# Products nobody reads, behind each group of gathered rows

## The reference

```python
msg = concat([h[src], h[dst]]) @ Mw.T + Mb
s1, s2 = segment_sum(msg, dst), segment_sum(msg * msg, dst)
mx, mn = segment_max(msg, dst), segment_min(msg, dst)
mean = s1 / deg;  var = relu(s2 / deg - mean * mean);  std = sqrt(var + 1e-30)
agg = concat([mx, mn, std, var])
u = concat([h, agg, agg * (logd / 4), agg * (4 / logd)]) @ Uw.T + Ub
u = batch_norm(u * sqrt(1 / N))
h = leaky_relu(u @ mix_w.T + mix_b, 0.01) + h
h = elu(layer_norm(h))
```

## Time and profile before

| | us |
|---|---|
| median of 3 runs | 2159.31 |
| lowest and highest of them | 2149.97, 2159.78 |
| span of the profiled execution | 2141.7 |
| PE busy, share of the span | 682.6, 32% |
| DVE busy | 1096.6, 51% |
| ACT busy | 455.6, 21% |
| POOL busy | 1235.7, 58% |

### The profile page before, as it was taken

How to read it: one execution, slowest core, us unless ns; L and a number is a source line. 1 busy time by engine, 2 the same in 40 slices (tenths; PEclk the granted TensorE clock), 3 DMA queues, 4 the chain that set the end, 5 groups by cost and what they waited for, 6 DMA issues and landing times. The chain is left out here.

```text
span 2141.7 us, 10446 instructions
## 1 busy us (share of the span) xinstructions
PE 682.6 (32%) x2156; PEld 402.8 (19%) x2156; DVE 1096.6 (51%) x2178; ACT 455.6 (21%) x1024; POOL 1235.7 (58%) x1358
## 2 busy tenths in 40 slices
PE   5611233132322470323132232362113322233265
PEld 5311121011111230112111111131101211112122
DVE  8600755464644843445464463572525664466464
ACT  0103321122111154111111111136101221112125
POOL 7673666676666127745675675406756666576504
PEclk9975666565655685566565666686556666656677
DMA  4363333333333033323332232204323333333200
GB/s 59 105 167 113 93 103 103 91 99 92 92 91 91 18 112 113 111 66 99 96 101 76 88 103 75 65 27 145 106 84 101 93 88 93 88 103 96 76 0 30
DMA packets 97107, 190.18 MB, mean 89 GB/s; under 512 B 30792, under 2 KB 56984, under 8 KB 97040
## 3 DMA queue, kind: packets, MB, share of 16 engines
q0 software_dynamic: 59968, 160.78, 26.6%
q1 hardware_dynamic: 37077, 28.77, 4.9%
HBM read 168.75 MB, written 17.75 MB: 87 GB/s over the span
## 5 line engine op out<-in xcount | busy, mean ns | idle before, releaser
L742 POOL DMA_INDIRECT G<-p_by_rank,index x774 | 734.8, 949 | 560.2 <-issue 227.8
L742 POOL DMA_INDIRECT G<-p_by_node,index x387 | 367.4, 949 | 225.0 <-issue 120.3
L921 PE MATMUL ps<-wide_ident,agg 128*128 128x128 f32 x288 | 80.3, 434 | 1209.3 <-issue 701.2
L1470 DVE TENSOR_TENSOR ps<-ps,G 128x1024 f32<-128x1024 f32 (+3 forms) x222 | 250.3, 1127 | 191.2 <-issue 78.4
L921 PEld LDWEIGHTS ps<-wide_ident,agg 128*128 128x128 f32 x288 | 51.5, 217 | 1239.5 <-issue 721.9
L936 PE MATMUL ps<-w_u_sb,aggT 128*128 128x384 f32 x576 | 284.3, 654 | 0.0
L1714 DVE SCALAR_TENSOR_TENSOR var<-tot,rdeg,msq 128x128 f32<-128x128 f32 x75 | 26.1, 348 | 426.4 <-ACT msq L1109 407.8
L936 PEld LDWEIGHTS ps<-w_u_sb,aggT 128*128 128x128 f32 x576 | 162.6, 282 | 144.7 <-issue 119.1
L1135 ACT ACTIVATE u_sb<-ps 128x128 f32<-128x128 f32 x75 | 20.7, 277 | 721.1 <-remote 509.0
L1472 DVE TENSOR_TENSOR ps<-ps,G 128x512 f32<-128x512 f32 (+3 forms) x222 | 141.6, 638 | 0.0
L1471 DVE TENSOR_TENSOR ps<-ps,G 128x512 f32<-128x512 f32 (+3 forms) x222 | 141.5, 637 | 0.0
(11 more groups left out here) (280 smaller groups left out, 1328.3 us busy)
## 6 DMA issues: line engine op xcount, KB each, us to landing
G<-p_by_rank,index POOLq DMA_INDIRECT x774
p_by_rank<-base SPq DMA_DIRECT2D x18, 512.0 KB
G<-p_by_node,index POOLq DMA_INDIRECT x387
p_by_node<-G SPq DMA_DIRECT2D x6, 514.0 KB
w_u_sb<-in_w_u SPq DMA_DIRECT2D x3, 768.0 KB
x_r<-rows_by_rank SPq DMA_DIRECT2D x1, 1600.0 KB
G<-shared_rows SPq DMA_DIRECT2D x12, 53.0 KB
windows<-src_pad SPq DMA_DIRECT2D x1, 624.8 KB, 14.1
```

The costliest lines, as they stand in the source:

```text
L742: g.indirect_dma_start(G[:, n % R, j, 0:w], None, table, bass.IndirectOffsetOnAxis(ap=named, axis=0))\
L921: ins = nc.tensor.transpose(ps[:, 2, i * D:(i + 1) * D], agg[:, t % 2, i * D:(i + 1) * D], ident[:, :])
L1470: TT(run[:, 0:nk, :], run[:, 0:nk, :], G[:, n % R, 0:nk, 0:2 * D], ALU.add)
```

## The change

Behind each group of a tile, from the tile's second group on, PE waits until the groups ahead of it are used (`dve_used`), and then runs two products of the identity with the first 512 columns of `hT`, into bank 2. Nobody reads them. This is done for tiles 1 to 23 of each layer, ahead of `turn(t)`. Before the first of them PE waits until ACT has copied the previous tile's turned aggregates out of bank 2, which `turn(t)` waited for already.

```diff
+            def kept_awake(l, t):
+
+                for n in tile_groups[t][1:]:
+                    pe.wait_ge(dve_used.sem, dve_used.at(l, n))
+                    for _ in range(2):
+                        mm(ps[:, 2, :], ident[:, :], hT[:, 0:4 * D], start=True, stop=True)
+
...
                     if l == 0 and t == AT[-1] + 1:
                         rank_bounds()
+                    if 1 <= t < T - 1:
+                        pe.wait_ge(agg_copied.sem, agg_copied.at(l, t))
+                        kept_awake(l, t)
                     if t <= FAR:
                         turn(l, t)
```

## The result

The changed kernel takes 2223.68 us (median of 4 runs, 2215.13 to 2230.2), the kernel before beside it 2156.62 (4 runs): ratio 1.0329, 95% interval 1.0275 to 1.0383. It is 67 us slower; 146 us were forecast. The profiled execution took 2223.51 us and its span is 2221.8, 80.1 longer than the span of before.

The account below looks back on a forecast made before the run. The prediction took POOL to bound the gather stage, its stops being the loss; 137 us for tiles during gathers plus 9 us for the tail, 146 us on 2159.31, gave about 2305 us, range 2195 to 2390 (8 in 10: 2120 to 2440).

Parts of the forecast that it names:

- The price, 2.8 us an instruction while gathers run: On PE, once it is behind: each product instruction costs about 2.8 us until reported, whatever its width.
- the one over 14 instructions (2.82): At a layer's start: 39.43 us between two reports, read as 14 product instructions at 2.82 us each.
- The release 5.3 us after POOL stops: At a POOL stop: PE's held update is reported 5.3 us after POOL's last gather ends.
- After a release 15 are free, then 7.5 plus one for each 2.8 us of gathering.: PE's queue: 15 instructions are reported without hold after a release, then 7.5 more plus one per 2.8 us of gathering.
- A round is now two tiles, and POOL stands 12.0 to 13.2 us in each: 6.3 us for a tile.: Gather stage: POOL stops once every two tiles, costing 6.3 us a tile instead of 3.9; chance 0.66.
- The term of 137 us: Tiles 2 to 20, taken while gathers run: 2.4 us more for each of 19 tiles in three layers, 137 us.
- The tail's 9 us: Tiles 22 and 23, after the gathers: their idle products add some 3 us a layer, 9 us in all.
- Rival 1: PE kept busy is not held, so POOL's stops end: faster, about 1900 to 1950 us; chance 0.17.
- Rival 2: Idle products are not counted or always hidden: same time, 2145 to 2165 us; chance 0.12.
- Rival 3: Rounds of one tile, a POOL stop in each: slower still, about 2640 us; chance 0.05.
- the 140 us: Expected sign in the profile after: POOL's waits for DVE grow by about 140 us in all.
- The first turn after each resume is reported some 15 us after PE issued it: Expected sign on PE: the first turn after POOL resumes, free before, is reported some 15 us after its issue.

Follow-up runs that it names:

- run 6: The changed kernel with all idle products of a tile issued at once behind the copy of the turned aggregates: 2226.45 us, ratio 1.0363 to the kernel before.
- run 9: The changed kernel with its idle products only in tiles 22 and 23: 2159.58 us, ratio 1.0053 to the kernel before.
- run 11: The kernel before with a bf16 update, plus four bf16 idle products where the change has two float32 ones: 2185.45 us, ratio 1.0169.
- run 8: The kernel before with gathers in layers 1 and 2 fetching rows of half the length, as many gathers: 2156.56 us, ratio 1.0034.

## Why the prediction was right in kind and wrong in size

*The price, 2.8 us an instruction while gathers run.* Right while a hold lasts, at 2.70 with 512-column idle products, 2.68 with the float32 update halved and 2.67 with four of six in bf16; the run with 32 columns puts most of the loss on the number of instructions.

Of the prediction's readings of this price the one over 14 instructions (2.82) doesn't count: the report at 927.60 comes 6.0 us after POOL's last gather ended (944.75 less 23.18 is 921.57), so it can be the release and not the last of 14 steps.

```profile
944.75 0.94 POOL L742 DMA_INDIRECT G<-p_by_rank,index  x1 [23.18 <-DVE ps L1472]
```

*The release 5.3 us after POOL stops.* Right in kind; in the changed kernel's six stops the first report comes after 4.3 to 8.0 us in five, and after 2.9 in the one that the steps reached by themselves.

*"After a release 15 are free, then 7.5 plus one for each 2.8 us of gathering."* This is the step that failed. With the change 26 instructions issued after the resume were reported by +15.4 (+11.3 to +32.3 over the six rounds, and +52 was forecast), in run 6 about 30 by +18.3. The one delay from which 7.5 was worked out (the 14th instruction at +18.45) fits as well a slack in time, however many instructions fall in it: the last of them was issued by +14.6, so only one or two steps of 2.8 us are in it, and the hold would have begun at about +13. One row could not tell the two apart. The other rounds of the kernel before could have warned me: the same update comes there at +13.4, +21.9, +16.2 and +16.9 after the resumes at 944.75, 1000.82, 1072.74 and 1233.97, where a fixed count would give nearly one time.

*"A round is now two tiles, and POOL stands 12.0 to 13.2 us in each: 6.3 us for a tile."* Wrong in consequence. The update that was to come at +52 came at +15.4 in the round shown and held nobody there. The hold is that of the next tile's turn (issued +22.8, reported +60.1; +48.6 to +69.0 in the six rounds), so a round is 2.5 tiles, as before. The term of 137 us, 2.4 for a tile, is in the same stretch 1.1 for a tile (5.0 less 3.9), 63 us over 57 tiles; POOL's waits for DVE measure +70.2.

*The tail's 9 us.* Right in the sum: 11 in run 9, 12.5 in the wait for the table; but most of it lies in layer 0.

*Rival 1, a PE kept busy is not held.* Refuted: ACT's two waits together rose from 680.7 to 849.0 us, and from none to four idle products the time only rose. The Trainium skill (TensorE: Matmul & The Clock Gate, section Why this matters for your kernels) advises against idle gaps between matmuls. The trace agrees that the granted clock rises, 0.661 to 0.733 and 0.796 with four products, and the time rose with it; the clock was not what the tiles waited for.

*Rival 2, idle products are hidden or not counted.* Refuted by the ratio. *Rival 3, rounds of one tile.* Not with the change; with four idle products some rounds come near it (18 gathers, 1.2 tiles), and its price, a full stop in each, was not seen.

*What was to be seen.* ACT's waits grew at the copy of the turned aggregates and shrank at that of the update, where I had both grow. POOL's waits rose by half of the 140 us. "The first turn after each resume is reported some 15 us after PE issued it" is wrong: it comes within 2 us of its issue, and it is the turn behind the forecast's update that comes late, 20 to 37 us after its issue.

*What stays open.* What opens a hold. A fixed time does not fit: of the changed kernel's own updates the one issued by +12.5 in the round above is 3.0 us late, that by +13.7 after the resume at 1273.30 is 18.6 us late, and that by +21.4 after the resume at 1029.27 is only 3.2 us late. A fixed count does not fit either, by the spread above. So that 7.5 instructions is wrong is shown, and what stands in its place is not. And why the bf16 update gains 62 us where the same count of float32 instructions gains 27: the price between reports is the same, and the shorter instruction (514 against 789 ns mean on line 936's group) is a difference that run 11 shows to be worth something, but no run splits it. That POOL's issuing is the cause of the late reports is left over from run 8, not shown: no run slowed or thinned the issuing.

## What to carry to other kernels

Price an engine's extra instructions by what waits for its semaphores, not by its idle time: PE was idle for two thirds of the span, and 458 us of work that fits into its idle time cost 67 us, because the results behind it in the queue were reported later. Where reports come at a fixed step for each instruction, cut the instructions: one bf16 instruction in place of a float32 product's two, in the update, made the kernel 2.9% faster, if its precision will do. And do not fit a queue's slack to one row; when a model is built on a slack, work out the forecast for a slack in time as well as in number, and let the range hold both.

## What the runs showed of the hardware

While POOL issues indirect gathers and PE is held, its results are reported late by about 2.7 to 2.8 us an instruction (27.28 us for 10 of 384 columns, 43.23 for 12 of 512 and 4 of 128, 16.04 for 6 of which 4 are bf16), read or unread; halving the bytes gathered changes the time by 0.3%. After the gathers resume there is a stretch with little or no delay, which differs from round to round: 26 instructions were reported by +15.4 us in one round and 31 by +18.3 in another, and in a third an update issued by +13.7 came 18.6 us late. After the gathers stop, held results come out within 4.3 to 8.0 us. Idle instructions of 32 columns raise the time by 2.7% with the clock at 0.655, those of 512 columns by 3.3% with the clock at 0.733.
